# Summing the second level's states on TensorE, in the PSUM bank that its norm reads

## The reference, cut to what matters

```
def step(h, inp):
    da, dbx, c = inp
    h = h * da + dbx
    return (h, jnp.einsum('bdn,bn->bd', h, c))      # sum over the 16 states
...
y = ys.transpose(1, 0, 2) + xt * Dv
return _layernorm(y, g, be)                          # (y - mean) / sqrt(var + 1e-5) * g + be, over 128 channels
...
y2 = _ssm(fx2, ...) + flip(_ssm(flip(fx2, -1), ...), 1) + y2_   # the level of 256 positions
```

## Time and profile before

| | |
|---|---|
| median of 3 runs | 4168.5 us (4166.28 to 4173.96) |
| the profiled execution | 4172.75 us, its span 4171.0 us |
| busy, us of the span | POOL 3307.2, DVE 3275.1, PE 2972.9, ACT 2698.8 |
| mean granted TensorE clock | 0.855 |
| one image in the middle (its level 2 begins at 1985) | 245.9 us |

### The profile page before, as it was taken

The page is one execution under the profiler, slowest core; times in us unless marked ns, Lnnn a source line. Parts: engine busy times, 40 slices in busy tenths (PEclk is TensorE's granted clock), DMA queues, the critical chain, the costliest instruction groups (busy, mean ns, idle before and its releaser), DMA issues.

```text
span 4171.0 us, 53040 instructions
## 1 busy us (share of the span) xinstructions
PE 2972.9 (71%) x12620; PEld 1412.1 (34%) x12620; DVE 3275.1 (79%) x3975; ACT 2698.8 (65%) x6662; POOL 3307.2 (79%) x1908
## 2 busy tenths in 40 slices
PE   6968767786777778767767876777687677867511
PEld 3534323343333334333333433333343333433200
DVE  1068887888878878787887888788787878888787
ACT  4477766766766676676757666675777667666532
POOL 0069698896979979697997969799696988969798
PEclk8988888898888898888888988889898888988755
DMA  1035444453544545354553544455354444535444
GB/s 42 1 112 199 145 168 164 169 201 126 194 157 164 176 153 203 129 186 154 175 191 133 202 144 173 162 173 198 119 201 145 171 163 170 201 118 193 163 162 173
DMA packets 187275, 664.08 MB, mean 159 GB/s; under 512 B 22736, under 2 KB 24672, under 8 KB 186976
## 3 DMA queue, kind: packets, MB, share of 16 engines
q1 hardware_dynamic: 186976, 661.47, 45.7%
HBM read 639.76 MB, written 21.63 MB: 159 GB/s over the span
## 4 chain that ended last, share of the span: by engine, by line
issue 21%; DVE 20%; POOL 19%; ACT 18%; PE 15%; DMA 6%; DVEq 1%; POOLq 0%; SPq 0%; ACTq 0%
ACT diag L1064 9%; POOL bx L1322 9%; PE pconv L792 8%; DVE h L560 7%; DVE slot_c L551 7%; POOL y L1350 6%; DMA bb<-bc_rows 6%; ACT slot_b L1178 3%; POOL h L1345 2%; DVE rs L507 1%; PE pm L810 1%; POOL bx L1325 1%; DVE xn L485 1%; PE pm L835 1%; PE pm L834 1%
## 5 line engine op out<-in xcount | busy, mean ns | idle before, releaser
L792 PE MATMUL pconv<-pad,diag 128*128 128x464 f16 (+11 forms) x9408 | 2142.0, 385 | 439.4 <-ACT diag L1064 304.1
L792 PEld LDWEIGHTS pconv<-pad,diag 128*128 128x128 f16 x9408 | 942.2, 102 | 1609.7 <-issue 362.8
L1350 POOL TENSOR_TENSOR y<-y,h 128x1024 f32<-128x1024 f32 (+2 forms) x672 | 1326.0, 1973 | 200.9 <-DVE h L560 178.2
L1178 ACT ACTIVATE slot_b<-delta,nega 128x512 f32<-128x512 f32 (+1 forms) x1280 | 809.4, 640 | 995.7 <-DVE slot_c L551 959.9
L1322 POOL TENSOR_TENSOR bx<-bb,u 128x1024 f32<-128x1024 f32 x512 | 1221.3, 2385 | 0.0
L551 DVE TENSOR_TENSOR_SCAN slot_c<-slot_b,bx 128x512 f32<-128x512 f32 (+1 forms) x1024 | 953.8, 955 | 313.1 <-POOL bx L1322 219.1
L560 DVE TENSOR_TENSOR h<-slot_c,cb 128x512 f32<-128x512 f32 x1280 | 860.2, 673 | 23.7 <-POOL y L1350 23.7
L551 DVE TENSOR_TENSOR_SCAN slot_c<-slot_b,slot_c,bx 128x512 f32<-128x512 f32 x512 | 663.7, 1296 | 74.9 <-ACT slot_b L1178 18.7
L1064 ACT ACTIVATE diag<-id,chi 128x128 f16<-128x128 f16 x1568 | 499.4, 386 | 8.0 <-PE pconv L792 7.5
L1064 ACT ACTIVATE diag<-id,clo 128x128 f16<-128x128 f16 x1568 | 497.8, 386 | 0.0
L1345 POOL TENSOR_TENSOR h<-h 128x512 f32<-128x512 f32 (+3 forms) x384 | 365.9, 953 | 22.6 <-ACT y L1158 3.9
(11 more groups left out here) (171 smaller groups left out, 3121.5 us busy)
## 6 DMA issues: line engine op xcount, KB each, us to landing
bb<-bc_rows SPq DMA_DIRECT2D x592, 512.0 KB, 4.3
cb<-bc_rows SPq DMA_DIRECT2D x592, 512.0 KB, 4.2
xr<-in_x SPq DMA_DIRECT2D x16, 1024.0 KB, 4.9
out<-ob SPq DMA_DIRECT2D x16, 1024.0 KB
bc_rows<-rows SPq DMA_DIRECT2D x64, 64.0 KB, 3.4
w<-in_w SPq DMA_DIRECT2D x2, 256.0 KB
wc<-in_wc SPq DMA_DIRECT2D x2, 256.0 KB
bc_rows<-rows SPq DMA_DIRECT2D x16, 32.0 KB, 3.9
```

The costliest lines, as they stand in the source:

```text
L792: ins = nc.tensor.matmul(img(bank(pconv, k), W)[:, r0:r1, c0:c1], w, pad[:, t, part, 16 * k + r0 + dy:16 * k + r1 + dy, c0 + dx:c1 + dx], ...
L1178: ins = nc.scalar.activation(slot_b[:, o:o + w], delta[:, so + c:so + c + w], ACT.Exp, scale=nega[:, st, n0 + n:n0 + n + 1])
L1350: pool.tensor_tensor(yv, yv, src[:, 0] if len(src.shape) == 3 else src, ALU.add).then_inc(q_y.sem, 1)
```

## The change

`FLAT` names the products 2 to 9, all of level 2; `POOLED` is empty, so every line that asks for it does nothing and DVE weighs all products as before. For the products in `FLAT` POOL's `gather` is not called. In its place PE opens a sum in bank 0 of `pm` with the centring matrix times the start value of `y` (`flat_init`, unit 1), and adds each weighed product with four matmuls of 256 columns by the same matrix (`flat_add`), the first product of unit k in the middle of unit k's taps, the second in unit k+1. The bank then holds the centred sum that `norm_square` of norm 1 reads; `norm_centre` of norm 1 is gone. A place of `h` that held such a product is free when PE has read it (`p_y`) and no longer when POOL has. Since bank 0 is taken from unit 1 to norm 1, the sums of the group norm and all of norm 0 move to bank 1. `ROOM` takes taps out of units 1 to 4:

| | unit 1 | 2 | 3 | 4 | 5 | 6 to 12 | 13 | 14 to 32 |
|---|---|---|---|---|---|---|---|---|
| taps before | 5 | 5 | 6 | 5 | 3 | 18 | 1 | 43 |
| taps now | 4 | 3 | 3 | 3 | 3 | 20 | 2 | 48 |

By it ACT makes rows 5, 6, 7, 8 of the diagonals from units 5, 7, 9, 12 on (before 5, 6, 7, 9), and `conv_add` of the first half moves from unit 11 to unit 13.

```diff
+FLAT = range(2, 10)
+POOLED = ()
...
         def norm_psum(k):
 
+            if k == 0:
+                return pm[:, HALF:HALF + 2 * L3], pm[:, HALF + 2 * L3:HALF + 4 * L3]
...
+            def place_free(i, q):
+
+                if q - HR in FLAT:
+                    dve.wait_ge(p_y.sem, p_y.at(i, flat(q - HR)))
+                elif q >= HR:
+                    dve.wait_ge(q_y.sem, q_y.at(i, added(q - HR)))
...
+            def flat_init(i):
+
+                pe.wait_ge(y_init.sem, y_init.at(i, 5))
+                pe.wait_ge(ch_rows.sem, ch_rows.at(i, 4))
+                pe.wait_ge(ch_pos.sem, ch_pos.at(i, 4))
+                nc.tensor.matmul(bank(pm, 0).rearrange("p (d n) -> p d n", d=2), cen[:, :], y[:, :, L1:L1 + L2], start=True, stop=False)
+
+            def flat_add(i, q):
+
+                d = PRODUCTS[q][1]
...
+                    pe.wait_ge(q_pr.sem, q_pr.at(i, weighed(q)))
+                for n in range(4):
+                    ins = nc.tensor.matmul(pm[:, d * L2:(d + 1) * L2], cen[:, :], h[:, q % HR, n * L2:(n + 1) * L2],
+                                           start=False, stop=n == 3 and q == FLAT[-1])
+                ins.then_inc(p_y.sem, 1)
...
+                    if k == 1:
+                        flat_init(i)
+                    if 2 <= k < 6:
+                        flat_add(i, products_of(k - 1)[1])
+                some = (mid + hi + 1) // 2 if 1 <= k < 5 else mid
+                if j is not None:
+                    taps(j, mid, some)
+                if i is not None and 1 <= k < 5:
+                    flat_add(i, products_of(k)[0])
+                if j is not None:
+                    taps(j, some, hi)
...
             def norm_square(i, k):
...
+                if k == 1:
+                    act.wait_ge(p_y.sem, p_y.at(i, len(FLAT)))
...
                         for q in products_of(v):
-                            gather(i, q)
+                            if q not in FLAT:
+                                gather(i, q)
...
-for k, v in {0: -16, 1: 8, 2: 4, 3: 14, 4: 4, 6: 6, 10: 0, 11: -8, 13: -10, 14: -8, 15: -27, 16: -10, 17: -12, 19: -4, 20: -10, 22: 3, 23: 7,
+for k, v in {0: -12, 1: -16, 2: -24, 3: -16, 4: -24, 6: 2, 10: 0, 11: -8, 13: -10, 14: -8, 15: -27, 16: -10, 17: -12, 19: -4, 20: -10, 22: 3, 23: 7,
```

More of the change, by code:

```diff
@@ L83, in decay_banks, with added, flat @@
     return banks(products_of(u)[0])
+FLAT = range(2, 10)
+POOLED = ()
 def weighed(q):
-    return q + 1 if q < 2 else 2 * q
+    return q + 1 if q < 2 else 2 + 2 * sum(v not in POOLED for v in range(2, q + 1))
+def added(q):
+    return sum(v not in FLAT for v in range(q + 1))
+def flat(q):
+    return q - FLAT[0] + 1
 NHALF = 2 * (NP - 2)
 HALF_BANK = [banks(q)[p] for q in range(2, NP) for p in (0, 1)]
+DVE_HALVES = [half_at(q, p) for q in range(2, NP) for p in (0, 1) if q not in POOLED]
 def build(nc, a, bc, out):
@@ L299, in build @@
         q_pr = Count("q_pr", weighed(NP - 1))
-        q_y = Count("q_y", NP)
-        n_y = Count("n_y", 24)
-        n_yc = Count("n_yc", NN)
+        q_y = Count("q_y", added(NP - 1))
+        p_pr = Count("p_pr", len(POOLED))
+        p_y = Count("p_y", len(FLAT))
+        n_y = Count("n_y", 8)
+        n_yc = Count("n_yc", NN - 1)
         n_sq = Count("n_sq", NN)
@@ L537, in scan @@
                 dve.wait_ge(u_bx.sem, u_bx.at(i, k + 1))
[L538 to L541, removed]
+                if q in POOLED:
+                    if p == 0:
+                        place_free(i, q)
+                else:
+                    before = max((v for v in DVE_HALVES if v < half_at(q, p) and HALF_BANK[v] == b), default=None)
+                    if before is not None:
+                        dve.wait_ge(q_pr.sem, q_pr.at(i, 2 + DVE_HALVES.index(before) + 1))
                 start = 0.0
@@ L547, in scan @@
                 for o in range(b * HALF, (b + 1) * HALF, n):
-                    hv, av, bv = slot_c[:, o:o + n], slot_b[:, o:o + n], bx[:, k % 2, o:o + n]
+                    hv = h[:, q % HR, o:o + n] if q in POOLED else slot_c[:, o:o + n]
+                    av, bv = slot_b[:, o:o + n], bx[:, k % 2, o:o + n]
                     if d:
@@ L568, in products @@
                 late = halves_of(k - 1)[-1] if k > 1 else None
+                if late is not None and late[0] in POOLED:
+                    late = None
                 for q, p in halves_of(k):
@@ L571, in products @@
                         chunk_first(i, CHUNK_MID[k])
-                    same = late is not None and banks(late[0])[late[1]] == banks(q)[p]
+                    same = late is not None and q not in POOLED and banks(late[0])[late[1]] == banks(q)[p]
                     if same:
@@ L577, in products @@
                         weigh(i, *late)
-                    late = q, p
+                    late = (q, p) if q not in POOLED else None
                 if k == NU - 1:
@@ L1361, in unit @@
                 if i is not None:
+                    for q in products_of(k - 1):
+                        if q in POOLED:
+                            weigh(i, q)
                     if k + 1 < NU:
```

38 lines of the change are left out of this document (27 added, 11 removed).

## The result

| | before | changed |
|---|---|---|
| median of 4 runs each on one chip | 4170.8 us (4166.3 to 4174.0) | 4060.5 us (4054.7 to 4064.5) |
| ratio, 95% interval | | 0.9735, 0.9718 to 0.9752 |
| span of the profiled execution | 4171.0 us | 4056.2 us |
| mean granted TensorE clock | 0.855 | 0.886 |
| from one image's start to the next, mean of 13 in the loop | 246.7 us | 239.7 us |

What follows compares the result with a forecast made beforehand. DVE was taken as the limit at first, then held up by POOL's lag from level 2. 7.4 less 0.4 gave 7.0 us per image, 112 us over 16 images, hence 4057 us; range 4018 to 4112 us.

Steps and rivals of the forecast that it cites:

- What goes on POOL: Level 2: eight products of 2.9 us leave POOL, 23 us per image, about 366 us in all.
- first addition of level 1: POOL entering level 1: its first addition at 2028.7 instead of 2036.0, 7.3 to 7.4 us sooner, bounding the gain at 7.4.
- DVE in level 2: Units 1 to 5: a 1.56 us wait goes and chunk subtractions save 0.75 us, so unit 5 begins 2.3 us sooner.
- ACT up to unit 10: Units 5 to 8: ACT makes 4 half rows of diagonals instead of 6, 4.1 us; unit 10 begins 6.4 us sooner.
- Units 10 to 15: The 1.40 us wait for ACT before unit 14's chunk goes, making 7.8 us for DVE; POOL bounds it at 7.4.
- named as a chance: Second chunk's opening operation, 2.51 us beside POOL, 1.14 alone: counted as no saving; possibly another 1.4 us per image, 4035 us.
- PE's price: PE in level 2: four matmuls of 256 columns cost 2.0 us per product, 16 us per image, plus 1 us start value.
- the 0 for DVE's waits: Level 2: PE has about 7 us after it gets a product's last half, so DVE never waits for PE's reading.
- PE late in units 19 to 30: Five more taps, 6.4 us, fill PE in units 14 to 32; small matmuls one to three us late, costing 0.4 us.
- Rival 1: ACT in units 6 to 10 or PE in 19 to 30 holds most back: 2 to 5.5 us per image; chance 0.17.
- Rivals 2 and 3: First: all holes close, 8.5 to 10 us per image, chance 0.12. Second: nothing moves, within 8 us of 4168, chance 0.03.
- Rival 4: TensorE falls to half clock in level 2; two troughs of 20.5 us make it 3.5 us per image slower; chance 0.08.

Runs made afterwards that it cites:

- e4: Changed kernel with one of the four matmuls of each level 2 product, so the sum lacks three of four states: 4043.7 us, ratio 0.9707.
- e3: Changed kernel with ACT beginning rows 6, 7 and 8 of diagonals in units 6, 7 and 9 as before, taps unchanged: 4103.6 us, ratio 0.9841.
- e1: Changed kernel with POOL's level 2 additions put back in the old places, on constants into a scrap tile: 4142.5 us, ratio 0.9921.
- e2: Kernel before with the new table of taps (ROOM line) and nothing else: 4179.2 us, ratio 1.0020.
- e6: Changed kernel with the old table of taps (ROOM line): 4147.4 us, ratio 0.9949.
- e10: Changed kernel with ACT's three silu operations and POOL's product for sz moved from units 5 to 7 into unit 3: 4004.2 us, ratio 0.9604.
- e12: Kernel before with ACT's three silu operations and POOL's product for sz moved into unit 3, nothing else: 4167.2 us, ratio 0.9989.
- e9: Changed kernel with the taps of units 18 to 21 as 4, 3, 1, 2 instead of 3, 2, 2, 3: 4050.9 us, ratio 0.9722.
- e7: Changed kernel with the taps of units 18, 19, 20 as 4, 3, 0 instead of 3, 2, 2: 4095.2 us, ratio 0.9813.

## Why the prediction was right

4057 us were predicted, 4060.5 measured, inside the range; 7.0 us per image both times. The mechanism was right: POOL's lag goes, and the gain is cut short by ACT and by PE's lateness. That the sum agrees to a tenth is partly luck: it rests on one term that came out 1.0 us too large and one of 1.2 us that wasn't counted. By its steps:

- **What goes on POOL:** 366 us expected, 356 measured. DVE's wait of `h` for `y` is gone from the list, and POOL rests in level 2. Its first addition of level 1 was to come 7.3 to 7.4 us sooner: it runs at 1975.75, 43.86 us after unit 1, against 50.98, 7.1 us.
- **DVE in level 2:** unit 5 sooner by 2.3 us expected. In the image that the prediction read it is 2.1, on the mean only 1.3. That image is one of two kinds: in 8 of the 13 images of before the units 1 to 5 took 40.1 us, like there, and in 5 they took 38.9, but in those level 2 began 9.1 to 9.3 us after the image's start instead of 6.9 to 7.1, since DVE's product ahead of it (L530) took 4.50 us and not 2.33. In the changed kernel level 2 begins at 6.7 in all 13. This, which the prediction didn't count, is most of the 1.2 us in the last row but one. Counted from the image's start, unit 5 comes 2.4 us sooner on the mean. On the change's side 0.8 us of units 1 to 5 goes with PE's pause at the loop's turn (e4).
- **ACT up to unit 10:** 4.1 us expected beyond those of level 2, 4.1 measured. e3 takes them back by ACT's rows alone and e1 by POOL's work alone, as the prediction's account of two bounds has it.
- **Units 10 to 15:** 1.0 us expected, 0.9 measured. But it came another way. The wait for ACT in front of the chunk of unit 14 was to go; it fell from 1.2 to 1.0 us per image only, and the one for ACT's decays rose from 1.1 to 1.9. What got shorter are the operations of the chunk on DVE, 3.6 us per image before and 3.0 now. The one that opens the chunk of unit 14 took 1.15 us in place of 2.55 in the image shown, which the prediction had named as a chance for the chunk of level 2 only (there it still takes 2.51 us in this image). It does so in 3 of 15 images; in the others it takes 2.1 to 2.5 us, before 2.2 to 3.5.
- **PE's price:** 2.0 us per product expected.

```profile
1943.94 1.89 PE L906 MATMUL pm<-h,cen 128*128 128x256 f32 x8
1945.66 4.03 PE L832 MATMUL pconv<-pad,diag 128*128 128x450 f16 x18
1949.53 1.89 PE L906 MATMUL pm<-h,cen 128*128 128x256 f32 x8
```

  The next tap starts 1.72 us after the product: a seventh cheaper. No wait of DVE for it, no wait of `conv_add` in the loop. So the 0 for DVE's waits was right. What the prediction has no term for is PE's pause at each turn of the loop, with which 1 us per image goes (e4); its loss is contained in the 1.3 instead of 2.3 us in level 2.
- **PE late in units 19 to 30:** 0.4 us expected, 0.3 to 0.4 measured net, and by the way described: 2.0 us of lateness, of which POOL's former waits give back 1.7. Only the reason for the lateness was another. The prediction took PE to be full there; it works 59.7 of 63.0 us. PE stands still for DVE's `dg`, which it didn't before (its pauses there were 4.56 and 5.01 us, for `ex` and `xg`), falls to half clock, and has two taps between `kt` and `fi` where it had one. e2 shows that this comes with the table and not with the new matmuls, and e6, with the old table, has the old wait for `fi` (13.7 us).

Rival 1 had the right places, ACT and PE, but not the size. Rivals 2 and 3 fell, though e10 came just below rival 2's times with another edit on top. Rival 4, the half clock, fell as a forecast of the time. Its sum also took the whole trough of 20.5 us as a price for PE, although PE stood idle in most of it: from the tap at 2035.49 on the earlier trace rows the low clock cost it some 2.5 us, an estimate from that tap's 2.43 us and the 5.18 us of the next three, against 1.27 us for a tap. It was right in kind and wrong in place: the clock is 0.94 and 1.00 in level 2, where the prediction looked for it, 0.50 for the tap behind the pause at the loop's turn, and 0.50 behind the pauses of 5.94 and 2.80 us in units 16 and 19. The Trainium skill (TensorE: Matmul & The Clock Gate, HAM oscillation) warns of waits inside a loop of matmuls. The trace agrees at `kt`: 1.98 us in the kernel before, without a pause, and 3.65 us behind a pause of 2.80 us. The pauses before a product in level 2, 0.42 and 0.45 us long, left the clock at 1.00.

## What to carry to other kernels

Work taken from one engine is worth what the next bound allows, so the table of another engine's side work has to move with it: here the two halves of the change gave 0.5% and minus 0.2% alone, and 2.65% together. And when such a change leaves an engine idle in one stretch, look for work of the same engine further on that is ready by then: moving four operations into the new holes gave another 56 us, and without the holes it gave 3. Read more than one image before a term is sized. A wait that travels with its releaser (a round trip between two engines, like the one for `fi`) ate nothing of the gain ahead of it. And when a run with less work is meant to give that work's price, look at what else it changed: e4 took out three quarters of the matmuls, and with them a pause of 3.3 to 6.1 us at each turn of the loop.

## What the runs showed of the hardware

- TensorE stood still at each new turn of the hardware loop, 13 times, for 3.1 to 6.3 us, in the ten runs with 137 to 139 packets on the instruction queue q8, and not in the four with 19 packets (the kernel before, e2, e4 and e12). The first ten record 13644 matmuls or more, the four 12620 or 12876. That code is loaded again at each turn is an inference.
- The clock fell behind some pauses of one to three microseconds. The 32 small matmuls for `fi` took 3.77 us behind a pause of 0.38 us in the kernel before, 5.13 behind 1.18 us (e9, clock 0.71) and 7.06 behind 2.46 us (e7, clock 0.50), each after 10 to 13 us of nearly unbroken work. With no tap in place of one between the two products (e7 against e9) 5.13 became 7.06 us. Yet in the changed kernel pauses of 2.00 and 1.90 us (ending at 1982.22 and 2012.13) left the clock at 1.00, so the length of a pause alone doesn't tell.
- The operation that opens a chunk (two inputs, 512 columns) beside POOL's two-input operations took 1.15, 1.45, 2.06 or 2.5 us from one image to the next of the same execution. Probably what counts is where in POOL's instruction it starts; no run put that to the test. The scans of 512 columns show nothing of the kind: 1.21 to 1.30 us in every unit of every image.
- The steps from image to image vary by up to 5 us (236.7 to 241.4 in the changed kernel) though the program repeats exactly. In e4, without the pause at the loop's turn, 12 of 13 steps are 238.9 to 239.2 us.
